# The deformable gather and the recurrence beside it: fifteen steps an image, gates and normalisation folded in, half of the one-hots on ScalarE

## The reference, cut to what matters

```python
x = x + _L0_conv_ref(_ln_c(x), ...)                    # deformable conv: 8 groups, 9 taps, bilinear samples
t = t + _L0_ffn_ref(_ln_t(t), U_i, V_i, b_i, ...)      # recurrence along the tokens of each image
# _L0_conv_ref ends: out = sum over taps of samp * mask; return out @ w_out + b_out
# _ln_t: (t - mean) / sqrt(var + 1e-5), and then for every token t, all 8 images at once:
i_t = sigmoid(xi_t + h @ V_i); g_t = tanh(xg_t + h @ V_c); o_t = sigmoid(xo_t + h @ V_o)
c_new = h * c + i_t * g_t                              # xi, xg, xo = normed x @ U + b
h_new = o_t * tanh(c_new)                              # 1024 steps, each needs the one before
```

## Time and profile before

| | |
|---|---|
| median of 3 runs | 6639.47 us (6637.65 to 6648.09) |
| the profiled execution | 6636.56 us, its span 6634.7 us |
| this stage's gather and recurrence | from 817 to 4058 us of the span |
| busy in the whole span | PE 4895.0, PEld 4138.8, DVE 3986.9, POOL 2678.8, ACT 1536.8 us |
| granted TensorE clock, mean | 0.825 of full |

### The profile page before, as it was taken

How to read it: one execution, slowest core, us unless ns; L and a number is a source line. 1 busy time by engine, 2 the same in 40 slices (tenths; PEclk the granted TensorE clock), 3 DMA queues, 4 the chain that set the end, 5 groups by cost and what they waited for, 6 DMA issues and landing times. The chain is left out here.

```text
span 6634.7 us, 124900 instructions
## 1 busy us (share of the span) xinstructions
PE 4895.0 (74%) x44814; PEld 4138.8 (62%) x44825; DVE 3986.9 (60%) x10252; ACT 1536.8 (23%) x4354; POOL 2678.8 (40%) x2903
## 2 busy tenths in 40 slices
PE   4666498989999898989989777774351556770856
PEld 2333287989989898989989674333321556330855
DVE  3444497878878787878878424668953334231212
ACT  2333201111121111111111112423241221140632
POOL 1334386646656565646646100002314333006034
PEclk7555599999999999999999657987675777895978
DMA  1111243323323232323323000000021222031222
GB/s 46 47 55 55 73 154 103 100 82 108 106 86 108 84 108 84 108 82 109 108 83 109 9 1 0 3 2 0 0 73 60 68 67 60 9 86 51 63 58 70
DMA packets 290147, 444.13 MB, mean 67 GB/s; under 512 B 41364, under 2 KB 186903, under 8 KB 281495
## 3 DMA queue, kind: packets, MB, share of 16 engines
q1 hardware_dynamic: 273302, 404.25, 18.7%
q0 software_dynamic: 16384, 33.59, 1.6%
HBM read 340.35 MB, written 97.39 MB: 66 GB/s over the span
## 5 line engine op out<-in xcount | busy, mean ns | idle before, releaser
L847 PE MATMUL bank<-dg_table,dg_one_hot 128*128 128x144 bf16 x27648 | 1905.7, 227 | 53.3 <-DVE dg_one_hot L934 50.4
L847 PEld LDWEIGHTS bank<-dg_table,dg_one_hot 128*128 128x128 bf16 x27648 | 1824.5, 101 | 63.6 <-issue 36.2
L798 POOL TENSOR_TENSOR dg_products<-dg_products 128x576 f32<-128x576 f32 x512 | 728.4, 1423 | 865.6 <-DVE bank L923 829.8
L829 PE MATMUL bank<-dg_hidden,dg_v_w 128*128 128x8 f32 x6144 | 927.8, 272 | 86.2 <-DVE dg_hidden L926 86.0
L829 PEld LDWEIGHTS bank<-dg_hidden,dg_v_w 128*128 128x128 f32 x6144 | 853.0, 210 | 111.4 <-DVE dg_hidden L926 107.1
L945 DVE TENSOR_TENSOR dg_products<-bank,dg_weight 128x432 f32<-128x432 f32 x1536 | 869.8, 597 | 11.9 <-PE bank L847 8.6
L934 DVE TENSOR_SCALAR dg_one_hot<-dg_index,dg_own_cell 128x1152 bf16<-128x1152 bf16 x1026 | 660.8, 685 | 8.0 <-DMA dg_index<-cell_index 8.0
L886 ACT ACTIVATE dg_gates<-bank 128x24 f32<-128x24 f32 x1024 | 194.7, 190 | 1368.7 <-PE bank L829 1368.7
L919 DVE SCALAR_TENSOR_TENSOR bank<-dg_gates 128x8 f32<-128x8 f32 x1024 | 288.0, 281 | 330.5 <-ACT dg_gates L886 330.0
L826 PE MATMUL bank<-dg_gate_inputs,ident 128*128 128x24 f32 x2048 | 388.5, 270 | 61.0 <-ACT dg_gates L886 35.5
L800 POOL TENSOR_TENSOR dg_products<-dg_products 128x288 f32<-128x288 f32 x512 | 414.7, 810 | 40.1
(11 more groups left out here) (393 smaller groups left out, 7371.0 us busy)
## 6 DMA issues: line engine op xcount, KB each, us to landing
dg_index<-cell_index SPq DMA_DIRECT2D x513, 288.0 KB, 3.3
dg_table<-window_table SPq DMA_DIRECT2D x64, 1728.0 KB, 7.8
tap_weight<-df_weight SPq DMA_DIRECT2D x16, 1296.0 KB, 4.8
dg_weight<-tap_weight SPq DMA_DIRECT2D x64, 324.0 KB, 8.0
window_table<-df_windows SPq DMA_DIRECT2D x16, 864.0 KB, 3.5
ex_slot_inputs<-ex_slots_in SPq DMA_DIRECT2D x40, 256.0 KB, 3.2
ex_slots_in<-ex_slot_inputs SPq DMA_DIRECT2D x40, 256.0 KB
ex_slot_outputs<-ex_slots_out SPq DMA_DIRECT2D x40, 256.0 KB, 2.4
```

The source lines that it names most:

```text
L798: pool.tensor_tensor(by[:, 0:4, :], by[:, 0:4, :], by[:, 4:8, :], ALU.add).then_inc(s_add, 1)
L829: mm = pe.matmul(out[:, g * IMG:(g + 1) * IMG], wv[:, g, :], hs[:, bass.ds(at, 1), :].rearrange("c o w -> c (o w)"), start=False, stop=(g ...
L847: mm = pe.matmul(bank(g, m)[:, at * UNIT:(at + 1) * UNIT], hot[g % 2][c][:, tap * TILE:(tap + 1) * TILE], table[k][:, c, g, e, :], start=( ...
```

## The change

One step: the three V matmuls accumulate onto gate inputs that an identity matmul brings into PSUM for 16 steps at a time; the c gate comes first and has a tanh of its own, i and o get one real sigmoid in place; the o gate instruction is gone; one weigh stands between the cell and h. Order: an image has 15 slots of one step and 9 or 10 units (a tap and a cell half, 3 matmuls); after each phase's eighth image 8 steps (`rest`) go without gathers. The tail of an image, its normalisation and its gate inputs are cut into hops placed at fixed slots of the next image (`after`; those of a pair of images together) or of `rest`; `finish` is gone. Adding the hidden states to x goes to GpSimd (`residual`). The one-hot of the second 128 cells is made by ScalarE in two instructions, |index - cell| and relu(1 - that). There are three pairs of one-hots in place of two, and they are made two groups ahead; GpSimd's folds wait for counted one-hots. The diff, cut to its core:

```diff
+    SLOTS = 15
+    LEAD = TILE - IMG * SLOTS
+    BLOCK = 16
+    HELD = 3
+    def units_by(s):
+        return UNITS * (s + 1) // SLOTS                 # UNITS = 144
+    def hots_in(q, s):
+        first = 0 if s == 0 else s + 1
+        return [(G * q + 2 + n // 2, n % 2) for n in range(first, s + 2) if G * q + 2 + n // 2 < GROUPS]
+    def phases(slot, after, rest, step):
+        for j in range(TPI):
+            for b in range(IMG):
+                for s in range(SLOTS):
+                    slot(j, b, s, (j - 1) * TILE + b * SLOTS + s if j else None)
+                    if j or b:
+                        after(j, b - 1, s) if b else None
+            for s in range(LEAD):
+                rest(j, s, (j - 1) * TILE + IMG * SLOTS + s if j else None)
         for at in range(TILE):
-            step((TPI - 1) * TILE + at, at)
+            step((TPI - 1) * TILE + at)
...
+            # GpSimd, fold(q, g)
+                early = hots_by(q, 2 * g + 1) if g < G - 1 else hots_by(q + 1, 0)
+                if paced or g < G - 1:
+                    pool.wait_ge(s_hot, START + min(early, RING + GROUPS))
                 pool.wait_ge(s_product, START + AHEAD + TRIPLES * (n + 1))
...
+            # TensorE
+            def step(t):
+                pe.wait_ge(s_h, START + t)
+                if at == 0:
+                    pe.wait_ge(s_gx, START + NGX * (j + 1))
+                if at % BLOCK == 0:
+                    pe.matmul(c_bank[...], core.ident[:, :], gx[j % 2][:, CG, :, at:at + BLOCK], ...)            # 128 columns
+                    pe.matmul(io_bank[...], core.ident[:, :], gx[j % 2][:, 0:CG, :, at:at + BLOCK], ...)         # 256 columns
+                pe.matmul(now_c, wv[:, CG, :], hidden(t - 1), start=False, ...).then_inc(s_pre_c, 1)
+                pe.matmul(now_io[:, 0:IMG], wv[:, 0, :], hidden(t - 1), start=False, ...)
+                pe.matmul(now_io[:, IMG:IO], wv[:, 1, :], hidden(t - 1), start=False, ...).then_inc(s_pre_io, 1)
+            def project(q, b, j):
+                pe.wait_ge(s_copy, START + q + 1)
+                pe.matmul(turn_at, w_out[:, :], turned[q % 2][:, :], start=True, stop=False)
+                pe.matmul(turn_at, core.ident[:, :], own_tokens(b, j), start=False, stop=True)
+                pe.matmul(cent, w_cent[:, :], turned[q % 2][:, :], start=True, stop=False)
+                pe.matmul(cent, centring[:, :], own_tokens(b, j), start=False, stop=True).then_inc(s_out, 1)
+            # variance(pair): one matmul of 256 columns; gate(pair, n, g): three of 256 columns
+            def after(j, b, s):
+                hop = {7: "turn", 8: "project"}.get(s)
+                if b % 2:
+                    hop = {7: "turn", 8: "project", 9: "variance", 12: "gates", 13: "last gate"}.get(s)
+            # rest(j, s, t): step, then {2: "turn", 3: "project", 4: "variance", 6: "gates" and "last gate"}
...
+            # ScalarE
+            def step(t):
+                act.wait_ge(s_pre_c, START + t + 1)
+                act.activation(gate_c[:, :], now_c, ACT.Tanh).then_inc(s_gate_c, 1)
+                act.wait_ge(s_pre_io, START + t + 1)
+                act.activation(now_io, now_io, ACT.Sigmoid).then_inc(s_gate_io, 1)
                 act.wait_ge(s_cell, START + t + 1)
+                act.activation(tc[:, :], cell, ACT.Tanh).then_inc(s_tc, 1)
+            def store_x(q, b, j):
+                act.activation(own_tokens(b, j), turn_at, ACT.Identity, bias=b_out[:, 0:1]).then_inc(s_x, 1)
+                act.activation(sq[:, b % 2, :], cent_at[...], ACT.Square, bias=b_cent[:, 0:1]).then_inc(s_sq, 1)
+            def inverse_std(pair):
+                act.preload_act_table_set(LOG_EXP)
+                act.activation(flat, var_at, ACT.Ln, bias=...)                  # 256 columns
+                act.activation(flat, flat, ACT.Exp, scale=-0.5).then_inc(s_rstd, 1)
+                act.preload_act_table_set(SIG_TANH)
+            def distance(n):
+                act.activation(far[n % 2][:, :], index[n % RING][:, :], ACT.Abs, bias=minus_cell[:, 0:1]).then_inc(s_far, 1)
+            def one_hot(n):
+                act.wait_ge(s_gathered, START + AHEAD + TRIPLES * (n - HELD + 1))
+                act.activation(hot[n % HELD][1][:, :], far[n % 2][:, :], ACT.Relu, scale=-1.0, bias=1.0).then_inc(s_hot_far, 1)
+            def slot(j, b, s, t):
+                if t is not None:
+                    step(t)
+                for n, part in hots_in(IMG * j + b, s):
+                    one_hot(n) if part else distance(n)
...
+            # VectorE
+            def step(t, between):
+                dve.tensor_tensor(ig, now_io[:, 0:IMG], gate_c[:, :], ALU.mult).then_inc(s_ig, 1)
+                dve.tensor_tensor(cell, ig, hc[:, :], ALU.add).then_inc(s_cell, 1)
+                between()                                                       # one weigh
+                dve.tensor_tensor(now, now_io[:, IMG:IO], tc[:, :], ALU.mult).then_inc(s_h, 1)
+                dve.tensor_tensor(hc[:, :], cell, now, ALU.mult).then_inc(s_hc, 1)
+            # slot: step (with the first triple of the slot between), the other triple if there is one,
+            # the one-hot of the first 128 cells in every other slot; sum_window in two halves (slot 10, and slot 5
+            # of the next image); normalise(pair), 256 columns, at slot 11 of the next image
```

More of the change, by code:

```diff
@@ L34 @@
 LOG_EXP = "natural_log_exp_and_others"
+SIG_TANH = "sigmoid_and_others"
 def halves(b):
@@ L713, in gather_samples @@
     BANKS = 4
[L714 to L746, removed]
@@ L805, in fold @@
                 if g == 0:
[L806 removed]
+                    pool.wait_ge(s_sum, START + 2 * q + 2)
                 pool.wait_ge(s_add, START + 3 * n + 3)
                 pool.tensor_tensor(folded[k][:, g, :], by[:, 0, :], by[:, 8, :], ALU.add).then_inc(s_fold, 1)
[L810 to L815 removed]
@@ new lines, in slot, with after @@
+            def slot(j, b, s, t):
+                if t is not None:
+                    step(t)
+                for n, part in hots_in(IMG * j + b, s):
+                    if part:
+                        one_hot(n)
+                    else:
+                        distance(n)
+            def after(j, b, s):
+                hop = {7: "turn", 8: "project"}.get(s)
+                if b % 2:
+                    hop = {7: "turn", 8: "project", 9: "variance", 12: "gates", 13: "last gate"}.get(s)
+                mix(IMG * j + b, b, j, hop)
@@ new lines, in rest @@
+            def rest(j, s, t):
+                if t is not None:
+                    step(t)
+                q = IMG * j + IMG - 1
+                mix(q, IMG - 1, j, {2: "turn", 3: "project", 4: "variance", 6: "gates"}.get(s))
+                if s == 6:
+                    mix(q, IMG - 1, j, "last gate")
+            act.preload_act_table_set(SIG_TANH)
+            act.sem_inc(s_hot_far, RING)
+            act.wait_ge(s_centre, START + 5)
+            act.wait_ge(s_own, START + 2)
+            for n in range(2):
+                distance(n)
+                one_hot(n)
@@ L992, in _ @@
             dve.wait_ge(s_own, START + 1)
-            one_hot(0, 0, 0)
-            walk(dve, step, group, tail, finish)
-            add_hidden(TPI - 1)
-    norm.done()
+            dve.tensor_scalar(minus_cell[:, :], own_cell[:, 1:2], -1.0, None, ALU.mult).then_inc(s_own, 1)
+            for n in range(2):
+                one_hot(n)
+            phases(slot, after, rest, lambda t: step(t, lambda: None))
+            dve.wait_ge(s_res, START + IMG * TPI)
+            last = tokens[:, :, TPI - 1:TPI, TILE - BLOCK:TILE].rearrange("c b j t -> c b (j t)")
+            dve.tensor_tensor(last, last, hs[(TPI - 1) % 2][:, TILE - BLOCK:TILE, :].rearrange("c t b -> c b t"), ALU.add).then_inc(s_res, 1)
 def divisive_mixer(core, args):
```

394 lines of the change are left out of this document (236 added, 158 removed).

## The result

The changed kernel took 6534.19 us (median of 4 runs, 6526.39 to 6538.4), the kernel before 6639.55 us beside it: a ratio of 0.9838, 95% interval 0.9822 to 0.9853. The median is 105 us lower where 117 were forecast (6534 for 6522). The profiled execution, the fastest of the four, took 6526.39 us, 110.2 less than that of before. The sum came out near, but several of its terms did not, and they cancel: that nearness is luck.

The account below looks back on a forecast made before the run. TensorE was taken to bound the kernel beside gathers, a chain at a phase's end. Gains 95 + 18 + 6 - 2 = 117 us off 6636.6 gave 6520, as a median 6522; range 6440 to 6620.

Parts of the forecast that it names:

- The slot: Gathers plus one recurrence step: TensorE takes 2.47 us, the step's chain 2.15 us, so 0.3 us to spare.
- Rival 2: Step chain longer than its slot, through ScalarE's one-hot at 1.9 us or strided PSUM: about 6640 to 6690 us; chance 0.12.
- A phase: Each of phases 1 to 7 takes 361.4 us in place of 375.0, 13.6 less; seven make 95 us.
- The stand at a pair: TensorE waits 2.6 us for a late step at each paired normalisation, three times a phase: 7.8 us.
- The end: The eight steps without gathers closing a phase take 25.6 us in place of 32.8.
- the lead of the steps alone: Time up to the first lone step: 26.8 us, where it was 31.7; with 16 tokens added at the end, 6 us gained.
- Rival 1: Clock falls at the pairs' standing, 6.5 us each; 21 places cost 137 us, giving 6659; chance 0.10.
- Rival 3: Table switches cost twice their trace row, 1.28 us more per load: 82 us more, 6604; chance 0.08.
- Rival 4: Clock holds through the phase-end steps without gathers: 10 us a phase less, 6442; chance 0.12.
- Phase 0: Phase without steps: gathers gain 5 us (bounds 0 and 23), 18 us together with the lead.
- The lead: Phase 0's lead without steps: 19 us in place of 32.
- The steps alone: The 128 last steps: 0.08 us less each, 10 in all, eight blocks cost 10 more: 0, between -10 and +12 us.

Follow-up runs that it names:

- combined version: Changed kernel with both one-hots on VectorE, phase 0 folds not paced, step tiles moved and blocks ahead of the wait: 6127.54 us, ratio 0.9708 against the kernel before.
- Newton steps of 128x256: Changed kernel with the inverse deviation by eight wide VectorE instructions, no Ln, Exp or table load: 6328.22 us, ratio 1.0035 against the kernel before.

## Why the prediction was right, and where it was not

**The slot: right.** V passes at 1415.55, 1418.06, 1420.38, 1422.89 and 1425.39 are 2.46 us apart on the mean (2.47), with TensorE full. ScalarE's one-hot takes 1246 and 1159 ns (1.2 us). Rival 2 is out. Putting identity matmuls back cost 0.36 us a slot, so this saving is real: it is the change. But that run has two of them a step. For the one that the kernel before had I have only its 0.22 us; with 0.04 for the blocks that leaves an estimate of 0.18 us a slot, some 150 us over 840 slots.

**A phase: 358.2 us, the mean of the six periods between the loads at the phases' ends from 1440.61 to 3589.78, where I had 361.4.** The stand at a pair was forecast at 2.6 and is 2.4 to 2.6 us. Standing in the gathers is 9.9 us a phase in place of 15.2 (7.8 + 3.2 + 2.4 + 1.8): the waits for the last fold (2.4) and for ScalarE's copy (1.8) are absent, the three pairs make 7.1, and the late slots at the start of an image make 2.7. The end takes 24.6 us for 25.6. Slow clock in the gathers costs about 9 us for 6.5, of two kinds, below. I also counted the lead of the steps alone twice, 5 us: it is the last of the seven ends. So 101 us of forecast (95 and 6) stand against 126 measured (118.1 and 7.6).

**Rival 1, the clock at the pairs: the mechanism came and the price did not.** I gave it 0.10, with "dense work on both sides" against it, and each fall the whole 6.5 us of a phase's end. It happened at 19 of 21 pairs, but at 3.3 or 6.9 us of half clock, 1.7 or 3.5 us each: 49 us, not 137. The same oversizing hid it in the total: at a phase's end TensorE now works through the steps, and in five of six ends the clock is back 3.6 to 4.5 us after the gathers resume (0.58, then 1.00), in the sixth at once, where the earlier trace rows have it at 0.50 until past 1480. I held 6.5 us for that, and it is nearer 2. I had also read it from the slowest of the six ends of before: the clock came back 13.0 us after the gathers there, and 8.1 to 8.7 us in the other five. So of the 45 us that I held for slow clock behind seven ends some 10 came, against 49 us at the pairs that I had left out: that they nearly cancel is luck. The runs show the cause: without the loads, with one load, and with two loads but no one-hot ahead of them, the clock holds; with 4.9 us of standing and no load it falls.

**Rival 3: no.** The table load at 1369.29 starts 0.02 us behind the end of a running one-hot, and the Ln 1.29 us after it, as in the earlier trace rows. By ScalarE: Activation LUTs, What ACT_TABLE_LOAD costs, of the Trainium skill a drain of some 1.38 us would be added; this trace does not agree, behind work or behind none. The trace of before could have settled it: its load, too, starts 0.01 us behind the end of running work, not on an empty queue as I wrote:

```profile
1453.30 0.63 ACT L125 ACTIVATE norm_sq<-norm_cent 128x512 f32<-128x512 f32 x1 [0.92 <-DVE norm_cent L145]
```

**Rival 4: no**, the clock is 0.50 through the end of a phase.

**Phase 0: wrong.** The step that failed is "with one on VectorE the fold (3.43) plus the 0.6 in which the one-hot keeps it out is 4.0", and 5 us less from it. The 4.0 came (254.8 us for 64 groups are 3.98 each), but it is more than the 3.9 of before, so no gain could follow from it. The gathers took 5.6 us more, for two reasons. The new wait of a fold on VectorE's one-hot count was in the diff, and I priced it at one fold an image: without it the gathers take 233.9 us, 21 less than with it. And the normalisation and gate inputs of six images moved from the lead into these gathers, where TensorE now does 13 us of work that is no gather (lines 903 to 922) in place of 4 (859 and 862); I counted only what the lead wins by that. So without the wait the gathers are only 15 us shorter than before, and my bound of 23 was out of reach. The lead was right (19.4 for 19).

**The steps alone: wrong in one term.** The blocks cost 1.29 us each, 10 in all, as forecast. The step got 0.065 us longer where I had 0.08 less. The term "without the o gate the 0.28 becomes about 0.20" failed: i*g to the cell still takes 0.28, and the sigmoid to i*g went from 0.22 to 0.27. Moving the tiles between SBUF and PSUM did not change it. In the code, the two hand-overs of 0.27 and 0.28 us (the time from one instruction's start to its follower's on the same or another engine) have two semaphore waits ahead of the instruction, of which the second is the late one; those of 0.19 to 0.22 have one wait, or (h in the kernel before) two with the late one first. No run changed that alone, so it stays open.

**What the named part was worth.** One-hots on ScalarE freed VectorE, which was not the bound beside the steps, and lengthened ScalarE's queue just where the recurrence waits for it. Undone, it gives 63 us back in the stretch: TensorE's standing in the gathers of a phase goes from 9.9 to 7.5 us (17 us in seven), and some 50 us of slow clock go; the two make 67. Most of the price is the clock's. In phase 0, which has no steps, ScalarE's one-hots do pay: they save 9 us with the pacing (254.8 for 263.9) and 9 without it (233.9 for 243.1). In all the named part costs 54 us.

**The sum.** Against the forecast the phases and the end gave 25 us more, phase 0 with its lead 11 less, the steps alone 19 less and the start 2 less. So the total is 7 us short in the profiled execution, while three of its four terms missed by more than that.

## What to carry to other kernels

Before moving work to an idle engine, look for the place where that engine's queue is on a chain, and price the queue there, not its share of the span. When an engine stands a little on a dense path, price the clock behind it from an experiment, not from another place in the trace. And where two in-order engines pass a value, give it a whole slot more than their program order suggests: a value made "after slot n" by the late engine is wanted two slots on, not one.

## What the hardware showed that I had not expected

Stands of TensorE in one pair, one after another, and the clock granted in the 15 us behind them: 0.62 us, 1.00; 0.95 and 0.62, 1.00; 1.23, 0.31 and 0.70, 1.00 (in the combined version three of 21 such places at 0.89); 1.23, 0.77 and 0.71, mostly 0.89; 2.38, mostly 0.89 or 0.77; 1.24 and 4.93, half clock for 6.8 us. Between the third and the fourth, half a microsecond of standing decided over some 1.7 us of lost time in 17 of 21 places. But the stands do not settle it alone: the same 2.38 us was followed by anything from 1.00 (at two pairs) to 0.67 (at one). What else decides, no run here shows.

With the Newton steps of 128x256, a VectorE instruction that took 0.42 us in 80 places took 1.50 us in the 48 where it started while GpSimd's 128x576 addition was running.
